# Moving a few steps in a hand-written order: layernorm, the first ffn1 tile, half of ffn2T and a PSUM copy

## The reference, cut to what matters

```python
qkv = x @ w_qkv + b_qkv                       # 128 -> 3 x 128, heads of 8
scores = q @ k.T / sqrt(8)                    # causal, per batch and head: 512 x 512
attn = softmax(scores)                        # heads 0, 1, 2: a third of the keys each
attn = attn * mult / sum(attn * mult)         #   is weighted by 1.6, and normalised again
x1 = layernorm(x + (attn @ v) @ w_proj + b_proj)
h = relu(s0 * ([x1, -x1] @ W0)) * 2           # W0, W1, W2 are +1 or -1, from booleans
h = relu(s1 * (h @ W1)) * 2                   # 512 -> 512
out = layernorm(x1 + s2 * (h @ W2))           # 512 -> 128
```

## Time and profile before

| | |
|---|---|
| median of three runs | 918.93 us |
| profiled execution | 916.2 us |
| its span | 914.5 us |
| TensorE matmuls busy | 828.8 us, 91% of the span |
| VectorE busy | 621.7 us, 68% |
| ScalarE busy | 606.6 us, 66% |
| GpSimd busy | 525.7 us, 57% |
| chain of waits, by engine | PE 43%, DVE 31%, ACT 10%, issue 6%, DMA 4%, POOL 4% |

### The profile page before, as it was taken

The page is one execution under the profiler, slowest core; times in us unless marked ns, Lnnn a source line. Parts: engine busy times, 40 slices in busy tenths (PEclk is TensorE's granted clock), DMA queues, the critical chain, the costliest instruction groups (busy, mean ns, idle before and its releaser), DMA issues.

```text
span 914.5 us, 17053 instructions
## 1 busy us (share of the span) xinstructions
PE 828.8 (91%) x5696; PEld 434.6 (48%) x5696; DVE 621.7 (68%) x2617; ACT 606.6 (66%) x1091; POOL 525.7 (57%) x763
## 2 busy tenths in 40 slices
PE   4488899999999999999999999999999999999865
PEld 1133244546455554546455554546455554545344
DVE  3487487685958587685958587685958587775124
ACT  3026368677776777677776777676776777676843
POOL 4205146575757657575756657575756657475732
PEclk9559599999999999999999999999999999999998
DMA  5735544545353535545353535545354535400000
GB/s 105 88 44 65 68 58 63 68 50 85 44 80 46 75 49 77 65 50 81 48 79 47 74 51 61 81 49 84 42 79 49 76 37 70 62 2 25 24 1 24
DMA packets 65741, 53.18 MB, mean 58 GB/s; under 512 B 5014, under 2 KB 63350, under 8 KB 65654
## 3 DMA queue, kind: packets, MB, share of 16 engines
q1 hardware_dynamic: 63542, 49.72, 40.5%
q0 software_dynamic: 960, 1.58, 1.4%
q10 hardware_dynamic: 1152, 0.79, 0.6%
HBM read 9.24 MB, written 4.19 MB: 15 GB/s over the span
## 4 chain that ended last, share of the span: by engine, by line
PE 43%; DVE 31%; ACT 10%; issue 6%; DMA 4%; POOL 4%; SPq 1%; ACTq 0%; POOLq 0%; DVEq 0%
DVE max_ps L783 16%; PE bank_ps L1041 8%; PE bank_ps L1042 7%; PE max_ps L955 7%; PE av_ps L1014 6%; PE score_ps L979 5%; ACT full L642 4%; ACT e L650 4%; PE bank_ps L1089 3%; DVE rowmax L783 3%; DVE stats L842 3%; DMA stack<-parts 2%; POOL h_lo L519 2%; ACT h_hi L663 2%; PE bank_ps L1078 2%
## 5 line engine op out<-in xcount | busy, mean ns | idle before, releaser
L783 DVE CUSTOM_DVE_ANT_0 max_ps<-max_ps,future 128x512 f32<-128x512 f32 (+3 forms) x1024 | 475.2, 520 | 229.6 <-PE max_ps L955 225.8
L650 ACT ACTIVATE e<-score_ps 128x512 f32<-128x512 f32 x640 | 368.7, 614 | 251.7 <-PE score_ps L979 250.4
L955 PE MATMUL max_ps<-stack 72*128 72x512 bf16 (+3 forms) x1024 | 250.7, 315 | 20.6 <-DMA stack<-parts 12.7
L979 PE MATMUL score_ps<-stack 75*128 75x512 bf16 (+3 forms) x1024 | 246.2, 305 | 8.8 <-DMA stack<-rowmaxT 4.9
L511 POOL TENSOR_SCALAR_AFFINE_SELECT e<-e 128x512 f32<-128x512 f32 x256 | 159.9, 636 | 155.3 <-ACT e L650 155.2
L519 POOL TENSOR_TENSOR h_lo<-full,h_hi 128x512 fp32r<-128x512 f32 x119 | 151.8, 1276 | 96.2 <-ACT full L642 95.2
L1014 PE MATMUL av_ps<-e,vaug 128*25 128x512 f32 (+3 forms) x2048 | 179.0, 446 | 0.1
L955 PEld LDWEIGHTS max_ps<-stack 72*128 72x128 bf16 x1024 | 83.3, 100 | 151.8 <-issue 70.8
L783 DVE DVE_READ_ACCUMULATOR2_ANT rowmax<- 128x1 f32 x1024 | 145.9, 142 | 0.0
L979 PEld LDWEIGHTS score_ps<-stack 75*128 75x128 bf16 x1024 | 92.3, 99 | 80.0 <-ACT e L650 28.8
L1041 PE MATMUL bank_ps<-h_hi,w 128*128 128x512 f32 x256 | 109.0, 426 | 10.1 <-ACT full L642 9.4
(11 more groups left out here) (95 smaller groups left out, 726.4 us busy)
## 6 DMA issues: line engine op xcount, KB each, us to landing
stack<-parts SPq DMA_DIRECT2D x276, 128.0 KB
x_in<-in_L_attn_hidden_states SPq DMA_DIRECT2D x16, 256.0 KB, 15.5
x_res<-in_L_attn_hidden_states SPq DMA_DIRECT2D x16, 256.0 KB, 2.9
out_x<-res SPq DMA_DIRECT2D x16, 256.0 KB, 3.3
stack<-parts POOLq DMA_DIRECT2D x12, 128.0 KB, 12.5
stack<-rowmaxT ACTq DMA_DIRECT2D x32, 24.0 KB
e<-in_L_ffn_k SPq DMA_DIRECT2D x1, 256.0 KB, 3.4
e<-in_L_attn_c_attn_w SPq DMA_DIRECT2D x1, 128.0 KB, 2.8
```

What stands on the lines that cost most here:

```text
L650: nc.scalar.activation(e[g % 2][:, t, :], score_ps[:, t % 2, :], ACT.Exp, scale=SCALE).then_inc(exped, 1)
L783: return nc.vector.tensor_tensor_reduce(out=scored_block, in0=scored_block, in1=future[:, P * (T - 1 - qt):S], scale=1.0, scalar=NEG, op0= ...
L955: return nc.tensor.matmul(out_ap[:, col:col + width], st[0:QK_ROWS, h, 0, P * qt:P * qt + P], st[0:QK_ROWS, h, 1, 0:width], start=True, st ...
L979: return nc.tensor.matmul(out_ap[:, col:col + width], st[0:ALL_ROWS, h, 1, P * kt:P * kt + P], st[0:ALL_ROWS, h, 0, P * kt:S], start=True, ...
```

## The change

Five places of the order move; no instruction is added or taken away. TensorE fills ffn1_0 at (3,6) instead of (3,5), and ScalarE reads it at (3,7). The first two of ffn2T's four matmul pairs stand at (0,5), with the bank's claim, and the other two stay at (0,6). The first layernorm's statistics stand at (1,8), behind that step's maximum, and its variance at (1,9). GpSimd computes rstd and shift right in front of the scalings, which for the first layernorm is behind masks(1,2). ScalarE copies the first half's `av_ps` at (2,8) instead of (2,9).

```diff
--- before.py
+++ after.py
@@ -63,7 +63,7 @@
     ("ffn0_2", -1, (3, 0), (3, 1)),
     ("ffn0_3", -1, (3, 1), (3, 3)),
     ("rowmax0", 1, (3, 3), (3, 4)),
-    ("ffn1_0", -1, (3, 5), (3, 6)),
+    ("ffn1_0", -1, (3, 6), (3, 7)),
     ("ffn1_1", -1, (3, 8), (3, 9)),
 )
 PLACES_OF_END = (
@@ -85,7 +85,7 @@
 )
 BATCH_OF = {what: batch for what, batch, _, _ in PLACES}
 
-FFN2_STEPS = ((0, 6), (0, 6), (0, 6), (0, 6))
+FFN2_STEPS = ((0, 5), (0, 5), (0, 6), (0, 6))
 FFN2_STEPS_OF_END = ((1, 3), (1, 3), (1, 3), (1, 5))
 
 SPLIT_STEPS = {"x1T": (2, 6), "ffn0_0": (2, 9), "ffn0_1": (3, 0), "ffn0_2": (3, 2), "ffn0_3": (3, 3),
@@ -96,8 +96,8 @@
 
 NEGMAX_ROWS = ((3, 5), (1, 2))
 
-LN_STATS = ((1, 7), (2, 1))
-LN_VAR = ((1, 7), (2, 2))
+LN_STATS = ((1, 8), (2, 1))
+LN_VAR = ((1, 9), (2, 2))
 LN_STATS_OF_END = ((1, 2), (3, 4))
 LN_VAR_OF_END = ((1, 2), (3, 5))
 
@@ -110,7 +110,7 @@
 COPIES_IN_FRONT = 6
 
 SUM_STEPS = ((1, 3, 7, 7), (1, 3, 7, 7), (1, 3, 7, 7), (1, 3, 7, 7))
-SUMS_OUT = ((0, 8), (2, 9))
+SUMS_OUT = 8
 
 
 class At:
@@ -534,15 +534,13 @@
                 pool.wait_ge(rowmax_step, b.times(8, 4 * half + 3))
                 nc.gpsimd.tensor_tensor(lo, r, mid, ALU.subtract).then_inc(rowmax_step, 1)
 
-            def deviations(b, i):
+            def normalise_tokens(b, i):
                 pool.wait_ge(ln_step[i], b.times(4, 3))
                 nc.gpsimd.tensor_tensor(rstd[:, i, :], var_eps[:, i, :], minus_half[:],
                                         ALU.pow).then_inc(rstd_ready[i], 1)
                 pool.wait_ge(rstd_ready[i], b.times(2, 1))
                 nc.gpsimd.tensor_tensor(shift[:, i, :], neg_mean[:, i, :], rstd[:, i, :],
                                         ALU.mult).then_inc(rstd_ready[i], 1)
-
-            def normalise_tokens(b, i):
                 if last_batch(b):
                     return
                 pool.wait_ge(rstd_ready[i], b.times(2, 2))
@@ -569,11 +567,6 @@
                     b = n + 2
                     if live(b) and not (b.c == 0):
                         split(b, k)
-
-                def layernorm_rstd(i):
-                    b = n + (-2 if i else -1)
-                    if live(b):
-                        deviations(b, i)
 
                 def layernorm_out(i):
                     b = n + (-2 if i else -1)
@@ -601,11 +594,9 @@
                 bias_residual()
                 masks(1, 0)
                 masks(1, 1)
-                layernorm_rstd(0)
                 masks(1, 2)
                 layernorm_out(0)
                 masks(2, 0)
-                layernorm_rstd(1)
                 layernorm_out(1)
                 masks(2, 1)
                 low(0, 0)
@@ -680,7 +671,7 @@
                             rowmax_rows(n + 1, 0)
                         if (g, t) == NEGMAX_ROWS[1] and live(n):
                             rowmax_rows(n, 1)
-                        if (g, t) in SUMS_OUT:
+                        if t == SUMS_OUT:
                             if g == 0 and live(n + -1):
                                 sums_out(n + -1, 1)
                             if g == 2 and live(n):
```

## The result

The changed kernel took 925.91 us (median of 4 runs), the kernel before 919.33 beside it: a ratio of 1.0078, 95% interval 1.0052 to 1.0104. Measured again later it gave 1.0066 (1.0040 to 1.0092). So it is slower, by 0.7%, about half of what I had forecast (932 against 918.9).

A forecast was written before the change was run, and what follows sets the result against it. TensorE was taken as the bound, busy 49.59 of 51.49 us per iteration, losing time only where it stands still. Terms 6.2 + 7.5 = 13.7 us gave 929.9 from the profiled 916.2, named 932 against the median 918.9; range 919 to 939.

The forecast's parts named there:

- the layernorm hides: Rival, chance 0.12: x1 under 0.76 us late, x_lo stays put, copy fits ScalarE's gap, ffn1_0 gains 0.14; 923.0 us.
- The q wait: ffn2T's first matmuls at (0,5) wait for ScalarE to empty q's bank: 0.44 us in 14 iterations, 6.2 us.
- Layernorm, copy and ffn1_0: Late x1, pushed av_ps copy and later ffn1_0 together make (3,7) 0.50 us late in 15 iterations: 7.5 us.
- what such an unbroken sequence costs the second layernorm shows: 3.56 us: GpSimd's rstd, shift and four scalings in a row take 3.56 us, making the first layernorm's x1 1.15 late.
- VectorE's total stays the same: Moving statistics and variance behind maxima leaves VectorE's summed work unchanged, so its max of (2,0) ends where it did.
- threshold of 0.76: Slack in us between ScalarE's second read of x1T and VectorE reaching x_lo; x1 later than this delays ffn0_0.
- The compounding rival: Rival, chance 0.10: late x_lo is held by a GpSimd scaling, about 0.36 us per iteration, 5.4 us more; 938 us.
- The copy pushed by late exps: Late x1T delays three exps on ScalarE, so the moved av_ps copy ends late; ffn0_0 read at 505.34, not 504.69.
- ffn1_0 behind exp(3,4): Scores of (3,6), now ahead of ffn1_0, wait for ScalarE's exp(3,4), which runs behind `full`, delaying ffn1_0 and (3,7).
- Head and tail add nothing: The kernel's start and end cost no extra time: end tables unchanged, and without exps no queue in the way.
- The signs I named: Trace signs: period about 52.4 us, q wait about 0.4, x_lo waiting for `full`, x1T over 1, ffn1_0's wait moving to scores(3,6).
- The period of 51.6: Sign against the forecast: an iteration period under 51.6 us would mean the predicted layernorm delay was wrong.

The follow-up runs named there:

- the layernorm alone: Kernel before with only the first layernorm moved: statistics at (1,8), variance at (1,9), rstd and shift behind masks(1,2); 917.12 us, ratio 0.9986.

## Why the prediction was right or wrong

- *Direction and range:* right; 924.5 to 925.9 lies between 919 and 939, though just under the forecast's own 926 to 937. Size: 13.7 us forecast, 6.8 between the spans. Of two terms one was right and one was wrong in sign, so the direction rests on the first alone; the mechanism that came is that of the rival with 0.12, "the layernorm hides".
- *The q wait (6.2 us):* right in mechanism. 0.44 forecast, 0.50 to 0.52 measured. The excess is the restart: the matmul starts 0.14 behind the read's end where I took 0.05. The count was wrong: I asked for batches n-2 and n, but the bank is q's, of batch n+2, so it is 12 iterations and not 14. 12 x 0.51 = 6.1: that the product agrees with 6.2 is luck, two errors that cancel. It wasn't given back anywhere, as argued from VectorE's start at (0,8).
- *Layernorm, copy and ffn1_0 (7.5 us):* wrong. 0.50 per iteration forecast, -0.15 measured. The step that failed was "what such an unbroken sequence costs the second layernorm shows: 3.56 us". I read the difference between 2.17 and 1.75 as what it costs to follow shift directly; it was x_lo, which ran beside the second layernorm's scalings and never beside the first's. With 1.75 in its place, and var_eps 1.06 instead of 1.23 late, x1 is 0.60 late. "VectorE's total stays the same" was off too, by the 0.13 that it became shorter. My own threshold of 0.76 stood beside it, and the rival "the layernorm hides" gave 923.0 and (3,7) 0.14 early; measured were 924.5 to 925.9 and 0.16 early, so its mechanism held and head and tail, below, are the rest.
- *The port between VectorE and GpSimd:* I saw x_lo's 780 against 693 ns and called the contention 0.09 us. The earlier trace rows held the other half, one step away: 0.42 us on GpSimd's side. The Trainium skill, "SBUF — State Buffer", § SBUF: two separate sides, says that of a VectorE instruction with two SBUF inputs and a GpSimd instruction that reads SBUF whichever starts first holds the shared pair for its whole length; by that rule GpSimd loses up to the length of x_lo when it is second, and the trace agrees (0.43 of 0.69 us, in the one scaling listed right behind x_lo's start). I had weighed the rule only against the loser I was looking at. The compounding rival built on it didn't come: x_lo now starts first and pays nothing.
- *The copy pushed by late exps:* right in kind, too large in size (ScalarE reads ffn0_0 0.12 late where I had 0.65), since x1T was only 0.60 late.
- *ffn1_0 behind exp(3,4):* right in kind, too large in size. 0.34 forecast for it alone, 0.20 measured, 0.24 in the changed kernel; the wait of 0.50 ahead of scores(3,6) is there.
- *Head and tail add nothing:* wrong by about 2 us; iteration 1 has no backlog to hide x1T (shown by the layernorm alone), and the tail met the lower clock.
- *The signs I named:* the q wait (0.36), x1T waiting for GpSimd (0.70, not over 1), the exchange of waits at ffn1_0 came; x_lo waiting for `full` did not, and its absence told at once which term was wrong. The period of 51.6 was no such sign: with the layernorm hidden, my own terms give 51.49+0.44-0.14 = 51.79, and the measured 51.85 is above 51.6 though the layernorm's delay was wrong.

## What to carry to other kernels

Where a pattern repeats, measure the period of one marker instruction, not the time: it gave 0.02 us where the medians gave 2, and single edits then add up to the whole. Before a duration is carried from one place of a trace to another, look at what the *other* engines did beside it; a long twin is a neighbour's price until shown otherwise. Two edits that hide in the same gap must be costed together: here each gained alone, and one cost 0.10 beside the other.

## What the runs showed of the hardware

A VectorE instruction with two SBUF inputs (0.69 us alone) and GpSimd's scalings held each other: 0.09 us when it started inside a scaling, 0.43 for the scaling that came behind it; with one input in PSUM neither paid. VectorE's tiny 128x4 `tensor_scalar` took 0.72 and 0.68 us instead of 0.17 beside GpSimd's affine selects. The same pair stands beside GpSimd's scalings in the kernel before and takes 0.17 and 0.16 there (VectorE's timeline, and GpSimd's narrowed to the scaling in which the pair starts):

```profile
499.85 0.17 DVE L851 TENSOR_SCALAR neg_mean<-moments 128x4 f32<-128x4 f32 x1
499.93 0.16 DVE L852 TENSOR_SCALAR var_eps<-moments 128x4 f32<-128x4 f32 x1
```

```profile
499.55 0.45 POOL L551 TENSOR_SCALAR res<-res,rstd,shift 128x128 f32<-128x128 f32 x1
```

But that scaling ends at 500.00, only 0.15 us after the pair's start, and wherever the pair starts inside a scaling, in any trace, at most 0.16 us of the scaling are left. So whether a scaling would hold it isn't shown. GpSimd's rstd doesn't: in the one place of the changed kernel's trace where the pair starts inside an rstd, `neg_mean` starts at 856.76, 0.59 us before the end of rstd, and takes 0.17.

So two of the shortest instructions of a queue can cost 1.1 us when a neighbour's order changes. Why rstd lets them pass and the affine selects don't was not tried.
